# Local attention: value products in 128x64 tiles with a third value tile built by two transfers, and norms ahead of square

## The reference

```
h = shift_token(x); q, k, v = split(h @ wqkv)          # 8 heads x 64
q = l2norm(q) * qs;  k = l2norm(k) * ksc;  q, k = rotary_xpos(q, k)
# windows of 64 queries; each sees its own 64 keys and the 64 before
sim  = einsum('bhwid,bhwjd->bhwij', 8 * bq, bk);  masked outside i-64 <= j <= i
attn = softmax(sim);  o = einsum('bhwij,bhwjd->bhwid', attn, bv)
x = x + o @ wo
```

## Time and profile before

| | us |
|---|---|
| median of 3 runs | 2303.07 (2303.02 to 2311.46) |
| the profiled execution, its own time | 2294.92 |
| its span | 2293.1 |
| busy: PE / PEld / DVE / ACT / POOL | 2136.7 / 1585.6 / 1706.8 / 1801.0 / 1431.8 |
| mean granted TensorE clock | 0.978 |

### The profile page before, as it was taken

One profiled execution on the slowest core, in us unless ns is written; L12 is line 12 of the kernel. 1 busy time (PEld: TensorE's weight loads), 2 busy tenths in 40 slices (PEclk: granted clock), 3 DMA queues, 4 the chain that ended last, 5 costly groups with the idle time before them and its releaser, 6 DMA issues. The chain is left out here.

```text
span 2293.1 us, 67424 instructions
## 1 busy us (share of the span) xinstructions
PE 2136.7 (93%) x22342; PEld 1585.6 (69%) x22342; DVE 1706.8 (74%) x4362; ACT 1801.0 (79%) x6112; POOL 1431.8 (62%) x1432
## 2 busy tenths in 40 slices
PE   6997999998797999999999999898999999999999
PEld 4994666665795888854888854674788864788863
DVE  5565999996555899964899964675899963899964
ACT  4775999995676999973999973556999982999982
POOL 3663777774662888840888850671788850788850
PEclk8997999999899999999999999999999999999999
DMA  6111000000113000000000000000000000000000
GB/s 249 44 42 42 2 0 0 0 1 38 35 44 111 12 7 9 7 3 3 11 7 9 7 0 0 2 0 6 9 9 8 8 1 5 9 9 7 9 1 37
DMA packets 22568, 46.02 MB, mean 20 GB/s; under 512 B 5344, under 2 KB 13664, under 8 KB 22048
## 3 DMA queue, kind: packets, MB, share of 16 engines
q1 hardware_dynamic: 17440, 34.07, 4.4%
q0 software_dynamic: 4992, 10.23, 1.6%
HBM read 24.51 MB, written 11.40 MB: 16 GB/s over the span
## 5 line engine op out<-in xcount | busy, mean ns | idle before, releaser
L280 POOL TENSOR_TENSOR space<-space 128x512 f32<-128x512 f32 x256 | 325.8, 1273 | 270.4 <-DVE space L383 270.1
L275 POOL TENSOR_TENSOR space<-space 128x512 f32<-128x512 f32 x256 | 267.6, 1045 | 128.1 <-ACT space L316 127.6
L330 ACT ACTIVATE space<-psum,space 128x128 f32<-128x128 f32 x1024 | 337.0, 385 | 2.7 <-DVE space L374 2.7
L177 PE MATMUL psum<-big,space 128*128 128x256 f32 x1024 | 267.9, 384 | 7.3 <-issue 3.5
L269 POOL TENSOR_TENSOR space<-space 128x512 f32<-128x512 f32 x256 | 267.0, 1043 | 7.9 <-DVE space L354 7.3
L1008 POOL TENSOR_TENSOR space<-space 128x256 f32<-128x256 f32 (+1 forms) x256 | 221.9, 888 | 75.2 <-DVE space L1117 70.9
L374 DVE TENSOR_REDUCE space<-psum 128x4 f32<-128x512 f32 x256 | 177.1, 692 | 100.8 <-PE psum L192 96.5
L1053 ACT ACTIVATE space<-space 128x128 f32<-128x128 f32 (+1 forms) x512 | 226.1, 446 | 7.3 <-DVE space L1108 6.5
L330 ACT ACTIVATION_READ_ACCUMULATOR space<-psum,space 128x1 f32 x1024 | 201.8, 197 | 0.0
L177 PEld LDWEIGHTS psum<-big,space 128*128 128x128 f32 x1024 | 175.6, 191 | 29.6 <-issue 16.2
L677 ACT ACTIVATE big<-psum,wt 128x512 f32<-128x512 f32 (+1 forms) x96 | 65.4, 686 | 151.9 <-PE psum L654 151.9
(11 more groups left out here) (194 smaller groups left out, 5425.8 us busy)
## 6 DMA issues: line engine op xcount, KB each, us to landing
big<-early SPq DMA_DIRECT2D x1, 6944.0 KB, 27.9
rows<-space SPq DMA_DIRECT2D x16, 256.0 KB, 2.7
z<-token_y SPq DMA_DIRECT2D x16, 256.0 KB, 4.7
space<-z SPq DMA_DIRECT2D x64, 64.0 KB, 1.9
space<-z SPq DMA_DIRECT2D x64, 63.8 KB, 2.1
big<-late SPq DMA_DIRECT2D x1, 3114.0 KB, 13.7
x<-x_t SPq DMA_DIRECT2D x4, 512.0 KB, 6.0
x_final<-x SPq DMA_DIRECT2D x8, 256.0 KB, 2.0
```

Of the source, the lines that this page charges most:

```text
L177: ins = mm(qk_ps[:, t * T:(t + 1) * T].rearrange("p (n c) -> p n c", n=2), hT[:, k, t * P:(t + 1) * P], wq[:, 0:2, j, :], start=(t == 0), ...
L275: pool.tensor_tensor(x, x, rn[:, (j - 1) % 2, :].unsqueeze(2).to_broadcast([P, 8, LD]), ALU.mult).then_inc(scaled, 1)
L280: pool.tensor_tensor(t3[:, j % 2, :], t1[:, j % 2, :], t2[:, j % 2, :], ALU.add).then_inc(summed, 1)
L330: ins = act.activation(pr[:, j % 2, h, t * P:(t + 1) * P], s_ps[h][:, t * P:(t + 1) * P], ACT.Exp, bias=nm[:, j % 2, h, t:t + 1], accum_ou ...
```

## The change

Three things are changed in `local_attention`.

First, the value products use all 128 partitions as keys. A third value tile per head pair holds the keys of the middle window: its lower half is the lower half of tile 1, its upper half the upper half of tile 0. SP copies both halves from SBUF to SBUF after ACT has written tiles 0 and 1. The products then are 3 column ranges times 2 heads (6 products, 12 instructions) in 128x64 tiles, all in bank 6. The copy by ACT (L322) and the semaphore `o0_ready` are gone, and the addition on DVE (L391) becomes a plain copy out of bank 6.

Second, on ACT the norms (Ln and Exp of unit s-1) are issued ahead of the square of unit s, not behind it.

Third, on PE the `wo` product (L221) is issued behind the transposes L232, not ahead of them.

```diff
-    v_ps, ol = g.bank[2][:, 0:T], (g.bank[2][:, T:2 * T], g.bank[6][:, 0:T])
+    v_ps, ol = g.bank[2][:, 0:T], g.bank[6][:, 0:T]
...
+    v_mixed = [sem(f"v_mixed{j}") for j in range(CH)]
...
     def sync(sp):
+        def mix(s):
+            j = s % CH
+            sp.wait_ge(v_ready, S0 + s + 1)
+            sp.dma_start(v[0:WIN, j, 2, :], v[0:WIN, j, 1, :]).then_inc(v_mixed[j], 16)
+            sp.dma_start(v[WIN:P, j, 2, :], v[WIN:P, j, 0, :]).then_inc(v_mixed[j], 16)
...
             sp.dma_start(h[64:P, 1:T], z[64:P, 0:T - 1]).then_inc(h_there[b % 2], 16)
+            for s in range(max(0, CH * b - 5), CH * b - 1):
+                mix(s)
+        for s in range(CH * B - 5, CH * B):
+            mix(s)
...
                 pe.wait_ge(pt_ready, S0 + u + 1)
-                pe.wait_ge(v_ready, S0 + (s if not isinstance(s, int) else min(s, U)))
+                pe.wait_ge(v_mixed[j], V0 + 32 * b)
...
-                for spans in (((0, P, 0), (0, P + WIN, 0)), ((P, P, 1), (P + WIN, WIN, 1))):
-                    for r, (q0, n, tile) in enumerate(spans):
-                        rows = slice(r * WIN, (r + 1) * WIN)
-                        for h in range(2):
-                            ins = mm(ol[r][h * LD:(h + 1) * LD, q0:q0 + n], v[rows, j, tile, h * LD:(h + 1) * LD], pt[rows, j % 2, h, q0:q0 + n],
-                                     start=(q0 == 0), stop=True, skip_group_check=True)
+                for q0, n, tile in ((0, P, 0), (P, WIN, 2), (P + WIN, WIN, 1)):
+                    for h in range(2):
+                        ins = mm(ol[h * LD:(h + 1) * LD, q0:q0 + n], v[:, j, tile, h * LD:(h + 1) * LD], pt[:, j % 2, h, q0:q0 + n],
+                                 start=(q0 == 0), stop=True, skip_group_check=True)
                 ins.then_inc(ol_ready, 1)
-            u = s - 5
...
-                mm(z_ps, wo[:, c, :], oT[:, (j - 5) % 2, :], ...).then_inc(wo_ready, 1)
...
+                mm(z_ps, wo[:, c, :], oT[:, (j - 5) % 2, :], ...).then_inc(wo_ready, 1)
...
+            u = s - 1
+            if only is None and runs(u, U):
+                act.wait_ge(ss_ready, S0 + u + 1)
+                act.activation(lnn[...], ss[...], ACT.Ln, ...).then_inc(ln_ready, 1)
+                act.wait_ge(ln_ready, S0 + u + 1)
+                if at_least(u, 2):
+                    act.wait_ge(scaled, S0 + u - 1)
+                act.activation(rn[...], lnn[...], ACT.Exp, ...).then_inc(rn_ready, 1)
             if begins(s, only):
                 act.wait_ge(proj_ready, S0 + s + 1)
...
                 act.activation(sq[:, j % 2, :], qk_ps, ACT.Square).then_inc(sq_ready, 1)
...
-            u = s - 4
-            if runs(u, U):
-                act.wait_ge(ol_ready, S0 + u + 1)
-                if at_least(u, 2):
-                    act.wait_ge(o_ready, S0 + u - 1)
-                act.activation(o0[:, j % 2, :], ol[0], ACT.Copy).then_inc(o0_ready, 1)
...
-                dve.wait_ge(o0_ready, S0 + u + 1)
+                dve.wait_ge(ol_ready, S0 + u + 1)
...
-                dve.tensor_tensor(oT[:, j % 2, :], ol[1], o0[:, j % 2, :], ALU.add).then_inc(o_ready, 1)
+                dve.tensor_copy(oT[:, j % 2, :], ol).then_inc(o_ready, 1)
```

More of the change, by code:

```diff
@@ L112, in local_attention @@
     U = B * CH
-    S0, B0, H0 = turn * U, turn * B, turn * 16 * B
+    S0, B0, H0, V0 = turn * U, turn * B, turn * 16 * B, turn * 32 * B
     wq, wo, tab = g.l1_wqkv[layer], g.l1_wo[layer], g.l1_tab[layer]
     qk_ps, qkT_ps, pt_ps, z_ps = g.bank[0], g.bank[1], g.bank[5], g.bank[7][:, 0:T]
-    v_ps, ol = g.bank[2][:, 0:T], (g.bank[2][:, T:2 * T], g.bank[6][:, 0:T])
+    v_ps, ol = g.bank[2][:, 0:T], g.bank[6][:, 0:T]
     s_ps, s_pair, ls = (g.bank[3], g.bank[4]), g.bank_pair3[:, :, 0:T], g.bank_pair3[:, :, T:T + 2]
     sq, t1, t2, t3, ss, lnn, rn, qk, v, hT = (room[x] for x in ("sq", "t1", "t2", "t3", "ss", "lnn", "rn", "qk", "v", "hT"))
-    nm, rl, pr, pt, o0, oT = (room[x] for x in ("nm", "rl", "pr", "pt", "o0", "oT"))
+    nm, rl, pr, pt, oT = (room[x] for x in ("nm", "rl", "pr", "pt", "oT"))
     h_zero, proj_ready, sq_ready = sem("h_zero"), sem("proj_ready"), sem("sq_ready")
@@ L124, in local_attention @@
     p_ready, rl_ready, normed, ptp_ready, pt_ready = sem("p_ready"), sem("rl_ready"), sem("normed"), sem("ptp_ready"), sem("pt_ready")
-    vp_ready, v_ready, ol_ready, o0_ready, o_ready = sem("vp_ready"), sem("v_ready"), sem("ol_ready"), sem("o0_ready"), sem("o_ready")
+    vp_ready, v_ready, ol_ready, o_ready = sem("vp_ready"), sem("v_ready"), sem("ol_ready"), sem("o_ready")
+    v_mixed = [sem(f"v_mixed{j}") for j in range(CH)]
     wo_ready, z_ready, masked = sem("wo_ready"), sem("z_ready"), sem("masked")
@@ L204, in tensor_body @@
                     prev.free(pe, 6)
-                for spans in (((0, P, 0), (0, P + WIN, 0)), ((P, P, 1), (P + WIN, WIN, 1))):
-                    for r, (q0, n, tile) in enumerate(spans):
-                        rows = slice(r * WIN, (r + 1) * WIN)
-                        for h in range(2):
-                            ins = mm(ol[r][h * LD:(h + 1) * LD, q0:q0 + n], v[rows, j, tile, h * LD:(h + 1) * LD], pt[rows, j % 2, h, q0:q0 + n],
-                                     start=(q0 == 0), stop=True, skip_group_check=True)
-                ins.then_inc(ol_ready, 1)
-            u = s - 5
-            if runs(u, U):
[L215 to L221, removed]
+                for q0, n, tile in ((0, P, 0), (P, WIN, 2), (P + WIN, WIN, 1)):
+                    for h in range(2):
+                        ins = mm(ol[h * LD:(h + 1) * LD, q0:q0 + n], v[:, j, tile, h * LD:(h + 1) * LD], pt[:, j % 2, h, q0:q0 + n],
+                                 start=(q0 == 0), stop=True, skip_group_check=True)
+                ins.then_inc(ol_ready, 1)
             u = s - 3
@@ L233, in tensor_body @@
                 ins.then_inc(ptp_ready, 1)
+            u = s - 5
+            if runs(u, U):
+                c = (j - 5) % CH
+                pe.wait_ge(o_ready, S0 + u + 1)
+                if is_first(u):
+                    prev.free(pe, 7)
+                if c == 0 and at_least(u, CH):
+                    pe.wait_ge(z_ready, B0 + b - 1)
+                mm(z_ps, wo[:, c, :], oT[:, (j - 5) % 2, :], start=(c == 0), stop=(c == CH - 1), skip_group_check=True).then_inc(wo_ready, 1)
             if runs(s, U):
@@ L301, in scalar_body @@
                 act.activation(pt[:, j % 2, :, :].rearrange("p h n -> p (h n)"), pt_ps, ACT.Copy).then_inc(pt_ready, 1)
+            u = s - 1
+            if only is None and runs(u, U):
+                act.wait_ge(ss_ready, S0 + u + 1)
+                act.activation(lnn[:, (j - 1) % 2, :], ss[:, (j - 1) % 2, :], ACT.Ln, scale=float(2 ** 20), bias=g.tiny[:, 0:1]).then_inc(ln_ready, 1)
+                act.wait_ge(ln_ready, S0 + u + 1)
+                if at_least(u, 2):
+                    act.wait_ge(scaled, S0 + u - 1)
+                act.activation(rn[:, (j - 1) % 2, :], lnn[:, (j - 1) % 2, :], ACT.Exp, scale=-0.5, bias=g.tiny[:, 1:2]).then_inc(rn_ready, 1)
             if begins(s, only):
@@ L336, in scalar_body @@
                     act.wait_ge(ol_ready, S0 + s - 3)
-                act.activation(v[:, j, :, :].rearrange("p a b -> p (a b)"), v_ps, ACT.Copy).then_inc(v_ready, 1)
+                act.activation(v[:, j, 0:2, :].rearrange("p a b -> p (a b)"), v_ps, ACT.Copy).then_inc(v_ready, 1)
             others("scalar", act, s)
@@ L405, in free @@
     def free(eng, bank):
-        last = (rotated, qk_ready, o_ready, rl_ready, rl_ready, pt_ready, o_ready, z_ready)
+        last = (rotated, qk_ready, v_ready, rl_ready, rl_ready, pt_ready, o_ready, z_ready)
         eng.wait_ge(last[bank], B0 + B if bank == 7 else S0 + U)
@@ L758, in sb @@
             return held[name]
-        att = dict(sq=[2, 2 * T], t1=[2, 2 * T], t2=[2, 2 * T], t3=[2, 2 * T], ss=[2, 8], lnn=[2, 8], rn=[2, 8], qk=[2, 2 * T], v=[CH, 2, P],
-                   nm=[2, 2, 2], rl=[2, 2, 2], pr=[2, 2, T], pt=[2, 2, T], o0=[2, T], oT=[2, T], hT=[2, T], y=[2, len(HCH), W])
+        att = dict(sq=[2, 2 * T], t1=[2, 2 * T], t2=[2, 2 * T], t3=[2, 2 * T], ss=[2, 8], lnn=[2, 8], rn=[2, 8], qk=[2, 2 * T], v=[CH, 3, P],
+                   nm=[2, 2, 2], rl=[2, 2, 2], pr=[2, 2, T], pt=[2, 2, T], oT=[2, T], hT=[2, T], y=[2, len(HCH), W])
         ret = dict(hT=[T], turn=[2 * T], qk=[2, 2 * T], kz=[2, 4, T], vm=[2, 2, 4 * (P + SD)], vn=[P], kt=[P], st=[2, P], t1=[2 * T], t2=[2 * T])
```

11 lines of the change are left out of this document (removed).

## The result

The changed kernel takes 2317.4 us (median of four runs, 2316.05 to 2318.62) against 2304.4 us for the kernel before on the same chip: a ratio of 1.005, with an interval of 1.0028 to 1.0072. On a second chip it was 1.0061 (1.0046 to 1.0076). It is slower, as forecast, and inside the forecast's range, but by 13 us where the forecast had 29; 29 us would be a ratio of 1.0126, outside both intervals.

A forecast was written before the change was run, and what follows sets the result against it. A new loop through DVE and ACT was to set the step at 4.12 us instead of 4.015: per call 7.75 + 1.08 - 1.5 = 7.3, four calls +29, so 2303.1 + 29 = 2332 us, range 2305 to 2356.

The forecast's parts named there:

- The loop that the move closes: DVE's L381 to L366, then ACT's norms and square, back to L381: a new loop that sets the step.
- The norms loop: ACT L295 to L316, POOL's scaling, PE's transposes, back to L295: said to set the old step of 4.015 us.
- The loop's length: New DVE and ACT loop: 2.91 + 0.03 + 0.34 + 0.21 + 0.60 + 0.03 = 4.12 us, ends 4.08 and 4.15.
- the signs that were to show it right: Squares 33.0 to 33.3 us per eight steps, ACT idle some 0.4 ahead of L312, 0.03 hand-offs, PE idle ahead of L232.
- Slow steps: On ACT, L316 comes 0.42 and not 0.34 behind L312 in two of eight steps, making eight steps 33.12 us.
- the start: Step 1 of a call: L306 begins at 739.82 instead of 738.74, +1.08 us a call, or nothing if the ramp has slack.
- Dropping L322 "by itself worth nothing": ACT's copy takes 0.26 us a step outside the old loop; removing it alone gains nothing in the step.
- PE "would be 4.0": PE's own step, without its wait for POOL, goes from about 3.9 to 4.0 us, beside 4.12, costing nothing.
- The rival of the extra drain: PE sets the step with one more tile-shape drain: 3.97 to 4.05 us, 2292 to 2312 us total; chance 0.11.
- PE's third shape: A third tile shape between L192 and L209 on PE adds one more gap, 0.1 to 0.2 us, taken as 0.15.
- 128x64 tiles side by side: PE's L209 overlaps two tiles, needing at most 0.48 of 0.61 us; otherwise about 2400 or 2350 us, chance 0.08.
- The transfers: Two 32 KB transfers a unit on SP's queue land in 4 to 6 us, some 13 us available: cost 0.

The follow-up runs named there:

- e2: Changed kernel with the square put back ahead of the norms on ACT; calls -3.3 us, ratio 0.9994 to the kernel before.
- e10: Changed kernel with the output copied twice out of PSUM on DVE, first into unused memory; calls +92.1 us, ratio 1.0417 to the kernel before.
- e12: Changed kernel plus an unused 256-column SBUF-to-SBUF copy on DVE ahead of the output copy; calls +61.8 us, ratio 1.0268 to the kernel before.
- e1: Kernel before with only the norms moved ahead of the square on ACT, old value products kept; calls +31.4 us, ratio 1.0113.
- e11: Changed kernel with the wo product ahead of the transposes again on PE; calls +13.4 us, ratio 1.0057 to the kernel before.
- e9: Kernel before with only the new value products and transfers, wo still ahead of the transposes; calls +7.8 us, ratio 1.0037.
- e3: Changed kernel with DVE's output copy moved behind the next step's sum of squares; calls +6.7 us, ratio 1.0032 to the kernel before.
- e8: Changed kernel plus an unused 256-column SBUF-to-SBUF copy on DVE behind the output copy; calls +297 us, ratio 1.1291 to the kernel before.

## Why the prediction was right in kind and twice too large

In the order of its steps:

- **The loop that the move closes: right.** The squares of two steps are joined through DVE and the norms, the two hand-offs of 0.03 are there, and ACT and DVE wait for each other once a step. (The norms loop as the bound of before is read from rows; no run lengthened it.) e2 shows that the norms' position is the cause, e10 and e12 that the loop is paid one to one.
- **The loop's length: the step that failed.** The mechanism was right and its sum was too large, above all in the 0.37 from L391 to L354. I had 4.12 with 4.08 as the lower end; it is 4.06 to 4.07. Its terms in the two fences above: DVE 841.42 to 844.30 is 2.88 and not 2.91, because L355 follows L392 after 0.33, not the 0.37 that I took; the square is 0.58, not 0.60; the rest is as forecast (0.03, 0.34, 0.20, 0.03). I knew that the 0.40 of the earlier trace rows might be held by the exponentials, and had worked out 0.33, but went to the middle. The trace of before could have settled it (ACT, the same step):

```profile
841.28 0.23 ACT L330 ACTIVATION_READ_ACCUMULATOR space<-psum,space 128x1 f32 x1
```

It ends at 841.51, and L354 starts 0.03 later, at 841.54; in 255 of the 256 steps it starts 0.03 or 0.12 behind that end. So the 0.40 held a wait in every step. e10 gives the spacing without one as 0.34 and 0.33 behind its two copies. Between two ends of which one holds a wait for another engine, the end without it was the price. The 0.055 a step (about 0.03 of it L355, 0.02 the square, 0.01 the norms) are 0.44 us per eight, and with the forecast's 31 eights over the four calls 14 of the 15.5 us between the forecast's 29.3 and the 13.75 found; with 4.065 in place of 4.12 the forecast's own sum gives 15.7. So two of the signs that were to show it right failed by their size: the squares are 32.67 apart and not 33.0 to 33.3, and ACT's idle time ahead of L312 is 0.19 and not 0.4.
- **Slow steps: right.** Twice in eight L316 comes 0.41 and not 0.33 or 0.34 behind L312, and the step is 4.14. 6 x 4.065 + 2 x 4.14 = 32.67.
- **Where the 13.7 us lie, over four calls.** The 56 steps behind the first seven: (228.69 - 225.03) x 4 = +14.7, where the forecast's 1.00 per eight makes 28. The first seven: +3.2, where it had 4.3 for the start and 3 for steps. The drain: -4.1 (forecast -6). The start is smaller than I had it: the first steps of the first call take 4.33, 3.66, 4.20, 3.81 and only then 4.06; that DVE and ACT still have slack there is my reading, not tested.
- **Dropping L322 "by itself worth nothing": right for the step of before, wrong for the new one.** e1 costs 31.4 us and the same with the new value products (e11) 13.4. With the norms moved, L322 lies in the second loop; without it eight steps are 0.37 shorter, 11 of these 18 us with the first seven steps, and the drains of the four calls give the other 7. Of the 0.37, plain steps give little (4.08 against 4.065); the two slow steps of eight fall from 4.26 to 4.14, since in the second loop the reciprocal's later start (0.12 and not 0.03 behind the accumulator) comes on top of the late L316. The forecast never closed this second loop; it was not needed for the changed kernel, but without it the parts don't add up. By call time: values alone +7.8, norms alone +31.4, both 13.4 with wo early.
- **PE "would be 4.0": right, and closer than it looked.** With wo early (e9) it is 4.015, with wo late, as in the changed kernel, 3.97 in half of the steps (e2). The rival of the extra drain thus lay 0.1 or less under the true step; with a loop 0.1 shorter it would probably have set the step (no run shows that), so that the direction was right with little to spare.
- **PE's third shape costs 0.17: right** (0.15 taken). The Trainium skill's page "TensorEngine Tiling (Array Packing)", section "Key Properties", says that a change of tiling mode drains TensorE: the 0.59 against 0.42 agrees, and e9 is a kernel in which PE, with this gap in its step, reaches the end time.
- **128x64 tiles side by side: right.** L218 keeps 0.67 with 0.74 to the next start, 0.14 of which is the wait for POOL. **The transfers: right**, 1.8 us; no run takes them out alone, but e2 carries them and is no slower than before.

What stays open: why the square is 0.58 long in the eleven kernels that issue it behind the norms and 0.60 in before, e2 and e9; what sets the step of e3; why half of e2's steps are 0.07 or more longer than the others; and whether a second output bank would let e3 go below before's step, which wasn't tried, because it needs another division of PSUM. No kernel here is faster than the one before by more than the measurement can tell; e2 comes nearest (0.9994).

## What to carry to other kernels

When an instruction is moved past another on an in-order engine, write down every closed way through all engines that now holds both, add up start-to-start times and hand-offs, and compare the sums with the step; busy shares and idle gaps can't tell: DVE, idle for 0.5 of 4.08 us here, is inside a loop in which no time is free. A row in which an instruction may have waited for another engine is no price for it: take the spacing of a similar pair that shows no wait. And where the unchanged rest of a kernel scatters by more than the effect, compare a stretch that holds only the changed code.

## What the runs showed of the hardware

A DVE copy from SBUF to SBUF stood still while POOL added. In e12 (copy ahead of POOL's start) and in e8 (behind it), DVE and POOL:

```profile
843.13 0.28 DVE L388 COPY space<-cf 128x256 f32<-128x256 f32 x1
843.34 0.41 DVE L394 COPY space<-psum 128x256 f32<-128x256 f32 x1
...
843.38 1.27 POOL L287 TENSOR_TENSOR space<-space 128x512 f32<-128x512 f32 x1 [0.84 <-DVE space L384]
```

```profile
842.24 1.24 DVE L393 COPY space<-cf 128x256 f32<-128x256 f32 x1
843.40 0.17 DVE L355 RECIPROCAL space<-psum 128x4 f32<-128x4 f32 x1
...
842.07 1.26 POOL L287 TENSOR_TENSOR space<-space 128x512 f32<-128x512 f32 x1 [0.76 <-DVE space L384]
```

The same copy takes 0.28 alone and 1.24 behind POOL's start, ending 0.15 after POOL's addition does (842.07 + 1.26 = 843.33). So it does in 240 of the 256 steps of e8, and in the nine, all at the ends of calls, in which no POOL instruction is under way when it starts, the same copy takes 0.28 there too; being in the loop, it adds 1.18 to every step and 283 us to the kernel's calls. The copy from PSUM (L394, 0.41) ran beside POOL at its usual length, and so did the sums of squares (L367, 0.67). The Trainium skill's page "Advanced Engine Details and Errata", section "Mode Summary" of its "VectorE Performance Modes", says that VectorE's second SBUF port is shared with GpSimd and that two-port VectorE instructions and GpSimd's block each other. The 0.28 against 1.24 agrees, and adds a price; that this copy was a two-port one is not recorded in the trace.
